# Value products joined with the router's logits for six of eight chunks, and the fills around the first attention groups reordered

## What is computed

```python
xn = layernorm(x)
q, k, v = xn @ Wq.T + bq, xn @ Wk.T + bk, xn @ Wv.T + bv
z = softmax(q @ k.T / 16) @ v
gates = softmax(xn @ Wg.T); scores, inds = top_k(gates, 2); scores /= scores.sum()
y_all[e] = (silu(xn @ We_gate[e].T) * (xn @ We_up[e].T)) @ We_down[e].T
y = sum(y_all[inds] * scores)
shared = (silu(xn @ Ws_gate.T) * (xn @ Ws_up.T)) @ Ws_down.T
out = x + z + y + sigmoid(xn @ Wsg.T) * shared
```

## Time and profile before

| | us |
|---|---|
| median of 3 runs | 510.38 |
| lowest and highest | 509.88, 511.83 |
| the profiled execution | 509.88 |
| its span, first to last instruction | 508.1 |
| TensorE busy | 502.8 |
| VectorE busy | 402.9 |
| ScalarE busy | 279.9 |
| GpSimd busy | 197.9 |

### The profile page before, as it was taken

How to read it: one execution, slowest core, us unless ns; L and a number is a source line. 1 busy time by engine, 2 the same in 40 slices (tenths; PEclk the granted TensorE clock), 3 DMA queues, 4 the chain that set the end, 5 groups by cost and what they waited for, 6 DMA issues and landing times.

```text
span 508.1 us, 9935 instructions
## 1 busy us (share of the span) xinstructions
PE 502.8 (99%) x3411; PEld 461.3 (91%) x3411; DVE 402.9 (79%) x847; ACT 279.9 (55%) x466; POOL 197.9 (39%) x178
## 2 busy tenths in 40 slices
PE   8999999999999999999999999999999999999997
PEld 6898988888889999999999889999989898989897
DVE  6989457899997677677776288997969797887997
ACT  4787884246655465555555547473826454553652
POOL 0001021111005777777760370454363436262740
PEclk9999999999999999999999999999999999999999
DMA  8937176111213565786575740632253323121212
GB/s 303 411 133 281 79 288 243 42 54 33 62 63 109 179 190 181 228 305 205 188 153 137 249 137 21 199 112 63 85 159 122 83 62 84 33 78 47 82 55 74
DMA packets 31185, 71.27 MB, mean 140 GB/s; under 512 B 5313, under 2 KB 9793, under 8 KB 30113
## 3 DMA queue, kind: packets, MB, share of 16 engines
q1 hardware_dynamic: 23840, 51.80, 28.6%
q0 software_dynamic: 6864, 18.75, 14.4%
q10 hardware_dynamic: 432, 0.09, 0.1%
HBM read 43.34 MB, written 27.28 MB: 139 GB/s over the span
## 4 chain that ended last, share of the span: by engine, by line
PE 89%; DVE 7%; issue 2%; ACT 1%; DVEq 0%
PE ps L808 55%; PE ps L1018 11%; PE ps L948 7%; PE ps L814 6%; PE ps L1050 6%; PE ps L903 1%; PE ps L861 1%; PE ps L965 1%; DVE pT L1334 1%; DVE acc L1431 1%; PE ps L912 1%; DVE place_hot L1523 1%; DVE sil L1412 1%; DVE hT L1334 1%; DVE probs_f L1675 0%
## 5 line engine op out<-in xcount | busy, mean ns | idle before, releaser
L795 POOL DMA_INDIRECT rows_y<-ytab,slot x64 | 81.1, 1267 | 87.6 <-DVE acc L1690 67.9
L765 POOL DMA_INDIRECT blk_x<-rows,row x79 | 83.7, 1059 | 48.4 <-DVE row L1538 22.7
L808 PEld LDWEIGHTS ps<-vv,pT 128*128 128x128 f32 x768 | 94.6, 189 | 1.3 <-DVE pT L1334 0.3
L808 PE MATMUL ps<-vv,pT 128*128 128x258 f32 x768 | 95.6, 283 | 0.1
L808 PE MATMUL ps<-xT,shared_w 128*128 128x512 f32 x384 | 92.7, 394 | 0.4 <-DVE sil L1412 0.2
L808 PEld LDWEIGHTS ps<-xT,shared_w 128*128 128x128 f32 x384 | 70.7, 188 | 15.5 <-issue 0.8
L808 PE MATMUL ps<-qT,xbT_hi 128*128 128x512 f32 x256 | 79.1, 390 | 0.0
L1018 PE MATMUL ps<-expert_w,blk_xT 128*128 x474 | 66.0, 288 | 0.3 <-DVE blk_xT L1334 0.3
L1018 PEld LDWEIGHTS ps<-expert_w,blk_xT 128*128 128x128 f32 x474 | 58.9, 190 | 0.6 <-issue 0.6
L1322 ACT ACTIVATE probs_f<-probs_f 128x1024 f32<-128x1024 f32 x32 | 33.8, 1057 | 41.3 <-DVE probs_f L1675 41.2
L1128 ACT ACTIVATE scored_t<-ps 128x1024 f32<-128x1024 f32 (+1 forms) x33 | 32.4, 996 | 43.6 <-PE ps L808 39.4
(11 more groups left out here) (167 smaller groups left out, 858.2 us busy)
## 6 DMA issues: line engine op xcount, KB each, us to landing
ytab<-blk_y SPq DMA_DIRECT2D x40, 256.0 KB, 2.8
keys<-xT SPq DMA_DIRECT2D x8, 1024.0 KB, 6.1
stage_e<-in_experts SPq DMA_DIRECT2D x16, 384.0 KB, 3.1
rows<-xn SPq DMA_DIRECT2D x8, 512.0 KB, 3.2
xbT_hi<-keys SPq DMA_DIRECT2D x8, 512.0 KB, 6.2
xbT_lo<-keys SPq DMA_DIRECT2D x8, 512.0 KB, 7.3
out<-acc SPq DMA_DIRECT2D x32, 128.0 KB, 1.8
acc<-in_x SPq DMA_DIRECT2D x7, 512.0 KB, 9.2
```

The lines of the kernel that those rows point to most:

```text
L765: e.indirect_dma_start(out=blk_x[:, q, n, :], out_offset=None, in_=rows, in_offset=bass.IndirectOffsetOnAxis(ap=row[:, 2 * b + n:2 * b + n ...
L795: e.indirect_dma_start(out=rows_y[:, r, k, :], out_offset=None, in_=ytab, in_offset=bass.IndirectOffsetOnAxis(ap=slot[:, k, i:i + 1], axis=0),
L808: ins = e.matmul(dst, stationary(p, k), moving(q, k), start=(n == 0), stop=(n == total - 1))
```

## The change

In the shared stage, chunks 2 to 7 get a joint product of values and logits: for each of their 24 tiles, xT is the stationary operand and the moving one is `value_w`, 256 columns of Wv and the 18 of the router side by side (274 columns, 6 products, new step `vals`). ACT copies the 18 logits and the 256 values out of the bank, POOL makes high and low part, SP stores them in DRAM (`vals`), all through rings of three. In attention batches 1 to 3 load their values from there (`vals_load`). Chunks 0 and 1 (batch 0) make their logits alone in the same form (24 products of 18 columns for each chunk), and their values in attention as before. The turned form of the logits, its transposes, its copies and its addition are gone. The stores of xT are steps of their own (`keys_store`) and stand later.

At the start, `first_product` takes all products with the high part of the tokens before those with the low part and no longer waits for the low part first; the warm products are 14 instead of 16 and 2; the Silu table is loaded by a step of its own; the statistics of chunks 1 and 2 and the root of chunk 1 stand later, and the scaling of the variance is a step of its own (`variance`).

At the seam and in attention: heads (0,0) is done whole and one pair earlier, the values of (0,0) in two halves around the last blocks' hidden product; group 0 has heads (0,1) and values (0,1) as its only fills, its last pair of scores is copied in two halves, its expert rows are added at its end; every group from 1 to 6 has one heads step and no values; qT is two buffers of one group each.

```diff
-WARM = (16, 2)
+WARM = 14
...
-    steps += [("stats", 0), ("root", 0), ("weights_hi", 0), ("invert", 0), ("norm", 0), ("weights_lo", 0),
-              ("row_shift",), ("tokens_in", 0), ("stats", 1), ("weights_hi", 1), ("shift_copied",), ("weights_lo", 1),
-              ("weights_hi", 2), ("weights_lo", 2), ("bias_shift",)]
+    steps += [("stats", 0), ("variance", 0), ("root", 0), ("weights_hi", 0), ("invert", 0), ("norm", 0), ("weights_lo", 0),
+              ("row_shift",), ("tokens_in", 0), ("bias_shift",), ("weights_hi", 1), ("weights_lo", 1), ("silu_table",),
+              ("stats", 1), ("variance", 1), ("shift_copied",), ("weights_hi", 2), ("weights_lo", 2)]
...
-        0: ([("router_split",), ("root", 1), ("stats", 2)], [("weights_hi", 3), ("invert", 1)], []),
-        1: ([("norm", 1), ("weights_lo", 3)], [("logits", 0)], []),
+        0: ([], [("root", 1), ("weights_hi", 3), ("invert", 1)], []),
+        1: ([("norm", 1), ("weights_lo", 3)], [("value_split",)], [("keys_store", 0), ("stats", 2)]),
...
-        3: ([], [], [("stats", 4)]),
+        3: ([], [("logits", 0)], [("stats", 4), ("keys_store", 1)]),
...
+        10: ([], vals(2, 0, 1), [("keys_store", 3)]),
+        11: ([("expert_load", 1), ("variance", 4, 5, 6, 7), ("root", 4, 5, 6, 7), ("invert", 4, 5, 6, 7)],
+            vals(2, 2, 3),
             []),
...
+        16: ([], [*vals(5, 0, 1), ("tokens_in", 6), ("norm", 7)], [("keys_store", 5)]),
+        17: ([], [*vals(5, 2, 3), ("best_experts", 1)], [("keys_store", 6)]),
...
+        20: ([], vals(7, 0, 1), [("expert_split", 4)]),
+        21: ([], vals(7, 2, 3), [("best_experts", 3)]),
...
+    ahead = {g: split("heads", *divmod(g + 1, 2)) for g in range(1, GROUPS - 1)}
...
         if g == 0:
-            steps += [*split("heads", 0, 1), ("heads", 1, 0), ("tops", g), ("heads_split", 1, 0),
-                      ("values", 0, 1), *spread(g), ("values", 1, 0), ("less", new),
-                      ("values_split", 0, 1), ("less", new + 1), *spread_second(g), ("probs", new), ("values_split", 1, 0),
-                      ("less", new + 2), ("probs_hi", new), ("probs", new + 1), ("probs_hi", new + 1), ("probs_lo", new),
-                      ("less", new + 3), ("probs_lo", new + 1), *rows(new + 2), *rows(new + 3)]
+            steps += [("tops", g), *split("heads", 0, 1), ("values", 0, 1), *spread(g), ("less", new),
+                      ("values_split", 0, 1), ("probs", new), ("less", new + 1), *spread_second(g), ("probs_hi", new),
+                      ("probs", new + 1), ("probs_lo", new), ("less", new + 2), ("probs_hi", new + 1), ("less", new + 3),
+                      ("probs_lo", new + 1), *rows(new), *rows(new + 1), *rows(new + 2), *rows(new + 3)]
...
+                elif kind == "vals":
+                    t = CT * (a[0] - NATIVE) + a[1]
+                    r = t % VR
+                    e.wait_ge(vals_copied, t + 1)
+                    if t >= VR:
+                        e.wait_ge(vals_stored[r], 16 * (t // VR))
+                    e.tensor_copy(vals_out[:, r, HI, :], vals_f[:, r, :]).then_inc(vals_hi, 1)
+                    e.wait_ge(vals_hi, t + 1)
+                    e.tensor_tensor(vals_out[:, r, LO, :], vals_f[:, r, :], vals_out[:, r, HI, :].bitcast(F32),
+                                    ALU.subtract).then_inc(vals_lo, 1)
...
+            def first_product():
+
+                def part(dst, at, p, q, k, **ends):
+                    cols = slice((at * KD + k) * P, (at * KD + k + 1) * P)
+                    return e.matmul(dst, shared_w[:, p, cols], xT_of(0)[:, q, k, :], **ends)
+
+                dsts = [ps[:, 2 + at, :] for at in range(2)]
+                for k in range(KD):
+                    e.wait_ge(xT_hi, k + 1)
+                    for at in range(2):
+                        part(dsts[at], at, HI, HI, k, start=(k == 0), stop=False)
+                        part(dsts[at], at, LO, HI, k, start=False, stop=False)
...
-                    bank, at = turn_bank(("logits", c)), 0
-                    for k in range(KD):
-                        for q in (HI, LO):
-                            ins = e.matmul(ps[:, bank, :], router[:, k, :], xT_of(c)[:, q, k, :], start=(at == 0),
-                                           stop=(at == 2 * KD - 1))
-                            at += 1
-                    ins.then_inc(summed_t, 1)
-                elif kind == "logits_turn":
-                    c = a[0]
-                    e.wait_ge(logits_t_copied, c + 1)
-                    bank = turn_bank(("logits_turn", c))
                     for n in range(CT):
-                        ins = e.transpose(ps[:, bank, n * P:(n + 1) * P], logits_t[:, n * P:(n + 1) * P], ident)
-                    ins.then_inc(logits_made, 1)
+                        product(ps[:, bank, n * RC:(n + 1) * RC], lambda p, k: xT_of(c)[:, p, k, n * P:(n + 1) * P],
+                                lambda q, k: value_w[:, q, k, D:VRC], logits_made)
+                elif kind == "vals":
+                    c, n = a
+                    if n == 0:
+                        e.wait_ge(xT_lo, KD * (c + 1))
+                    product(ps[:, turn_bank(("vals", c, n)), 0:VRC], lambda p, k: xT_of(c)[:, p, k, n * P:(n + 1) * P],
+                            lambda q, k: value_w[:, q, k, :], valued)
...
+                elif kind == "vals":
+                    t, i = CT * (a[0] - NATIVE) + a[1], CT * a[0] + a[1]
+                    bank = before[("vals", *a)][0]
+                    e.wait_ge(valued, t + 1)
+                    copied(logits_sb[:, i, :], ps[:, bank, D:VRC], logits_copied)
+                    if t >= VR:
+                        e.wait_ge(vals_lo, t - VR + 1)
+                    copied(vals_f[:, t % VR, :], ps[:, bank, 0:D], vals_copied)
```

More of the change, by code:

```diff
@@ L38 @@
 RC = NE + 2
-RLO = 32
+VRC = D + RC
+VR = 3
+NATIVE = 2
+STORED = TILES - NATIVE * CT
 EPS = 1e-5
@@ L134, in down, with vals @@
         steps.extend(behind)
+    def vals(c, *tiles):
+        return [("vals", c, n) for n in tiles]
     shared = []
@@ L209, in plan @@
             steps.append(("blk_gate_up", b))
+        if b == PAIRS - 1:
+            steps.append(("heads", 0, 0))
         if b == PAIRS:
-            steps.append(("heads", 0, 0))
+            steps.append(("values", 0, 0))
         if 0 < b <= PAIRS:
             steps.append(("blk_hidden", b - 1))
+        if b == PAIRS:
+            steps.append(("heads_split", 0, 0))
         if b == PAIRS + 1:
-            steps.append(("values_first", 0, 0))
+            steps.append(("values_second", 0, 0))
         if b > 1:
@@ L243, in probs @@
         return [("probs", n), ("probs_hi", n), ("probs_lo", n)]
-    ahead = {1: split("heads", 1, 1), 2: split("heads", 2, 0), 3: split("heads", 2, 1), 4: split("heads", 3, 0),
-             5: split("heads", 3, 1), 6: split("values", 3, 1)}
-    behind = {2: split("values", 1, 1), 3: split("values", 2, 0), 4: split("values", 2, 1), 5: split("values", 3, 0)}
+    ahead = {g: split("heads", *divmod(g + 1, 2)) for g in range(1, GROUPS - 1)}
     def spread(g):
@@ L253, in spread_second @@
         return [("spread_second", g), *([("shift_in", g + 2)] if g + 2 < GROUPS else [])]
-    steps += [("keys_load", 1), ("shift_in", 0), ("shift_in", 1), ("heads_second", 0, 0), ("heads_split", 0, 0), ("ones",), *split("values", 0, 0)]
+    steps += [("shift_in", 0), ("keys_load", 1), ("shift_in", 1), ("vals_load", 1), ("values_split", 0, 0), ("ones",)]
     steps += [("gather", i) for i in range(YR)]
@@ L267, in plan @@
             steps += [("probs", new - 1), ("probs_hi", new - 1)]
-        steps += [("scores_max", g, 1), *(rows(new) if g == 0 else [])]
+        steps += [("scores_max", g, 1)]
         if g == 1:
@@ L273, in plan @@
         else:
-            steps += [*(weigh(old) if g else []), *scores(g, 2), ("scores_max", g, 2), *(rows(new + 1) if g == 0 else [])]
+            steps += [*(weigh(old) if g else []), *scores(g, 2), ("scores_max", g, 2)]
         steps += [*scores(g, 3), ("scores_max", g, 3)]
@@ L322, in __init__ @@
                 turn += 2
-            elif kind in ("logits", "logits_turn", "counts", "rows_map"):
+            elif kind in ("logits", "vals", "counts", "rows_map"):
                 banks = [(("turn", turn % 2), step)]
@@ L446, in build @@
         r_xr = r_w + 4 * 4 * KD * D + PART
-        qT = at("qT", r_ew, [P, 2, KD, NT], F32R)
+        qT = [at(f"qT{n}", where, [P, 2, KD, CHUNK], F32R) for n, where in enumerate((r_xr, r_ew))]
         vv = at("vv", r_ew + 4 * PART, [P, 2, 2, BT, VC], F32R)
@@ L588, in build, with copied_upto, tops_upto @@
         ROWS_LAST = 16 * (NCH // 2)
-        LAST_PAIR = (GROUPS - 1, CT - 1)
+        HALVED = ((0, CT - 1), (GROUPS - 1, CT - 1))
+        def copied_upto(g, pair):
+            return nth[("scores", g, pair)] + sum((g, pair) >= both for both in HALVED)
+        def tops_upto(g):
+            return 4 * (g + 1) + sum(g >= both[0] for both in HALVED)
```

(21 more changed lines are left out.)

220 lines of the change are left out of this document (115 added, 105 removed).

## The result

The changed kernel takes 515.97 us (median of four, 513.81 to 516.89) where the kernel before takes 510.33: a ratio of 1.0105, interval 1.0088 to 1.0121. The forecast was 507.5 with a range up to 510.5. The profiled execution took 515.99 us, with a span of 514.2 where the sum gave 505.2, so 9.0 us were missing from it.

The account below looks back on a forecast made before the run. TensorE was taken as the bound, with 89% of the chain. Terms -10.1 + 1.1 + 5.3 + 0.2 + 0.6 = -2.9 us, from a median of 510.38 to 507.5; range 503.8 to 510.5.

Parts of the forecast that it names:

- The price of a product of 18 columns: Logits of chunks 0 and 1: 0.111 us each, 48 products, 5.3 us; ends 1.9 and 5.8.
- The start, step by step: Start: first product 0.5 us earlier, fourth gate-up at 20.05 after a 1.1 us wait; +0.2 us, bounds -0.9 and +1.
- The fill of group 0: Between group 0's last scores and first weighing: 5.6 us of products go, 0.6 us of waits come, bounds 0 and 3.
- the rival of the late fill: Group 0: the chain misses by two VectorE steps and group 1 inherits the delay; 2.5 us more, 510.0; chance 0.17.
- The ring of three stores: Value stores in the shared stage: holds if a store lands within 5.9 us; taken as 0, bounds 0 and +7.
- The slow side's rival: Shared stage: value stores queue behind key and row stores and land in 7.7 us; +7.0 us, 514.5; chance 0.08.
- "Added": Term for the logits of chunks 0 and 1 alone: 48 products of 18 columns, +5.3 us.
- Rows 5: Profile rows used to price thin products: one-column fp32 at 0.111 us each, 16 fp16 loads with 80 columns below 0.039.
- "the statistics that move behind are hidden by the logits product": Start: the moved statistics lie beside the 2.7 us logits product that follows the fourth gate-up.
- "the later gathers take POOL out of the way ... I take 0 there": Group 1: VectorE is late by some 2.5 us after group 0's rows move behind, but this costs 0.
- "144 x 0.0076": Shared stage: 144 value products with 18 more columns take 0.1274 instead of 0.1198 us; +1.1 us.
- -7.6 (six turned logits): Shared stage: removing the turned logits of six chunks; for all eight, 8 x 1.26 = 10.1 us of TensorE.

Follow-up runs that it names:

- The kernel with the later rows: Changed kernel with the expert rows of tile 3 added in group 1 instead of at the end of group 0: ratio 1.0096 to the kernel before.
- The last kernel of the experiments: Against the kernel with turned logits for chunks 0 and 1 and statistics spread: value_split and statistics 6 and 7 put later; 507.15 us, ratio 0.9944 to the kernel before.
- the kernel with 128-column logits: Changed kernel with logits of chunks 0 and 1 made by products of 128 columns instead of 18: ratio 1.0056 to the kernel before.
- the repetition: The changed kernel measured once more, unaltered, beside its mended forms: ratio 1.0118 to the kernel before.
- the statistics spread: Against the kernel with turned logits for chunks 0 and 1: statistics 3 and 4 a step or more later, value_split ahead of step 6; ratio 1.0003 to the kernel before.
- the turned logits: Changed kernel with rows of tile 3 and statistics 2 later, and chunks 0 and 1 logits in the old turned form: ratios 0.9955 and 0.9968 to the kernel before.
- the kernel with the three mends: Changed kernel with 128-column logits for chunks 0 and 1, rows of tile 3 in group 1, and statistics 2 one step later: ratio 0.9969 to the kernel before.
- the kernel with the burst of 18 columns: Kernel before with 24 unused products of 18 columns added behind each of the first two chunks' logits: ratio 1.0106 to the kernel before.

## Why the prediction was wrong

**What held.** The price of a product of 18 columns: 24 take 2.67 and 2.60 us, 5.27 together, forecast 5.3. The Trainium skill, TensorE: Matmul & The Clock Gate, section LDWEIGHTS, was the rule that the trace agrees with (0.111 and 0.108 measured, 107 ns by the page); the 25 ns of its Back-to-back issue gap weren't, and that section says itself that its formula leaves no budget for the load of weights at small sizes. The start, step by step: the table loads stand at 11.03, 13.68 and 17.34, and the fourth gate-up starts at 20.10 behind a wait for `sil`, forecast 20.05; the wait is 0.63 us instead of 1.1, as the first product starts 0.31 us earlier and not 0.5, so part of that hit is luck. The fill of group 0: 22.1 us from the first scores to the first weighing, no wait before it, and the scores and the head behind it take 5.90 and 2.85 us instead of 5.46 and 2.73, 0.6 in all, as forecast, so the rival of the late fill is out in its place, though group 1 did inherit a delay of VectorE, from elsewhere. The ring of three stores: they land in 3.0 us (median; the longest took 5.8) against the 5.9 at which it would decide, and GpSimd waited for one twice, 1.2 us in all; ScalarE never waited for GpSimd there. The slow side's rival had the right sign and the wrong mechanism.

**What failed.** The first step is in "Added": the 48 products were priced by their own interval and nothing else, with the clock at 1.00 taken over from the windows of before. Their price was right, but behind them the clock falls to half for most of the next product: 3.2 us, shown with 18 against 128 columns at the same duration in two kernels. Rows 5 give no hint of it: both of their runs last under 1 us, and the 512-column products behind the fp16 one ran at a clock of 1.00. I put no bound above for it.

The second is "the statistics that move behind are hidden by the logits product". They do lie beside TensorE's work, but on VectorE statistics 2 stand ahead of the low part of chunk 1's tokens, for which that very logits product waits. I asked what hides them and not who queues behind them: 0.7 us. Together with the first, 3.9 of the 4.0 missing there.

The third is "the later gathers take POOL out of the way ... I take 0 there". I followed the four additions on VectorE, and not their buffers: with three of them GpSimd stands idle for 10.14 us before the fourth gather. 2.76 us on VectorE became 1.84 on TensorE and, in the profiled execution, 1.5 of clock. The kernel with the later rows shows 3.0 of the 3.6; 0.6 are not located.

The fourth is small, "144 x 0.0076": the joint products take 0.129 us each (132 of them between 50 and 108 us, from the start of a tile to that of the next row, without the tile ahead of a wait), not 0.1274, 0.2 us. And four turns of tokens that follow a value product wait, 1.1 us in all, for the copy of a bank, as the two turning banks now also serve the 24 value tiles. The view of these turns in the changed kernel, what ended their idle time (us, times), and one of them:

```profile
  ACT vals_f L1190: 1.1, 4
...
93.50 1.34 PE L887 MATMUL ps<-cf,xn 128*128 128x128 f32 x8
94.59 3.12 PE L1012 MATMUL ps<-shared_w,hT 128*128 128x256 f32 x24
```

93.50 to 94.59 is 1.09 us, where such a turn takes 0.80 without it. I priced what ScalarE has to do there as a sum over the stage and not copy by copy. The 32 products of these turns take 0.128 instead of 0.103 us, 0.8, and 0.2 us of wait stand ahead of one turn. With the 0.2 above that gives 1.2 where 1.0 is missing.

Is the sum right otherwise? The last kernel of the experiments answers it, as it has no fall of the clock. By my terms it is -7.6 (six turned logits) + 1.1 + 0.6 (waits of the fill), and its first down product comes 1.3 us earlier (29.93, 31.19 in the kernel before beside it): -7.2. Its span is 3.4 below (505.0, 508.4). Of the 3.8 between, 0.3 is the interval of the joint products (0.1295), 1.4 the turns (48 at 0.127 instead of 0.101, and 0.2 of wait ahead of one), 0.7 the wait for `value_w`, 0.6 the seam, 0.5 attention and 0.1 the fill; 0.2 stay open. So by my terms this form should have given 7 us, and it gave 3.4: each join costs a little.

## What to carry to other kernels

Where one engine's clock depends on what it does, price a new kind of product by the rows behind it too: a run of thin products, each with its own load of weights, can cost time behind it too (1.6 us behind 2.6 here), and widening them to 128 columns was free (2.60 and 2.63 us for 24). For each step moved, list who queues behind it on its engine and which ring's buffer it gives back, before asking what hides it. And a move that takes a wait away is worth a look at the same engine 15 us later: statistics taken out of one gap twice became a wait in the next, until they stood where VectorE had time.

## What the runs showed of the hardware

24 products of 18 columns with a load of 128 x 128 each, 2.6 us with TensorE and its weight loads busy and no gap, were followed by a granted clock of 0.50 to 0.58 in six cases of eight, and 24 of 128 columns with the same duration by 1.00 in six of six. The Trainium skill, TensorE: Matmul & The Clock Gate, Part 1: The HAM clock gate, says that activity of TensorE releases the throttle, and the section HAM oscillation names its idle gaps as what brings the throttle back. Here it came back without a gap. Behind waits it fell as well, but not each time: behind 1.84 us in group 1 (0.79 in 345:353) and 1.83 us in the kernel with 128-column logits, not behind 1.81 us in the repetition; behind 2.16 us with the statistics spread (0.59); not behind 1.43 us with the turned logits or 0.74 in the last kernel. Such a fall costs about 1.5 us. In the profile of the kernel with the three mends it was low at the start too (0.56 in 8:15), which no experiment explains. So a single execution can differ by one fall from the next.

The kernel before took 524 us in some runs and 510 in others, and one chip gave both at different times, so it isn't a matter of the chip alone. In the traces of all kernels here, from the first block product to the first scores it is 119.2 to 120.1 us in the short runs and 132.1 to 134.3 in the long ones, and the stretches behind it agree. The first 55 us from the first block product on, of the kernel with the burst of 18 columns (span 529.1) and of the kernel before at 510:

```profile
173.24:228.24 55.00, 49.78 (x404) 48.62 (x403) 35.33 (x80) 25.22 (x59) 36.90 (x36) 0.97 0.54 165
```

```profile
166.75:221.75 55.00, 54.64 (x468) 54.36 (x466) 40.68 (x93) 29.86 (x69) 42.51 (x42) 1.00 0.68 218
```

165 GB/s instead of 218, 404 products instead of 468, and TensorE idle for 5.2 of 55 us. For the three longest of these waits (3.20, 1.06 and 0.81 us) the profile names nothing that ended them, and what makes the stage longer in some runs is open.
